# A two-FFN and state-space layer: the shared expert takes its turned operands from memory, where the router's are stored

## What is computed

```python
x = x + 0.5 * _L0_ffn_ref(_layernorm(x, axis=-1), ...)
x = x + _L0_attn_ref(_layernorm(x, axis=-1), ...)
x = x + 0.5 * _L0_ffn_ref(_layernorm(x, axis=-1), ...)
```

```python
logits = flat @ router_w.T
scores = jax.nn.softmax(logits, axis=-1)
_, topk_idx = jax.lax.top_k(logits + router_bias, K)
...
xg = flat[tok_table]
g = jnp.einsum('ecd,efd->ecf', xg, gate_w)
u = jnp.einsum('ecd,efd->ecf', xg, up_w)
y = jnp.einsum('ecf,edf->ecd', jax.nn.silu(g) * u, down_w)
out = jnp.zeros_like(flat).at[tok_table.reshape(-1)].add((y * w_table[..., None]).reshape(-1, d))
sg = jnp.einsum('nd,sfd->nsf', flat, sh_gate_w)
su = jnp.einsum('nd,sfd->nsf', flat, sh_up_w)
out = out + jnp.einsum('nsf,sdf->nd', jax.nn.silu(sg) * su, sh_down_w)
```

## Time and profile before

| | |
|---|---|
| time, median of 3 runs | 2375.12 us (2374.70 to 2375.79) |
| profiled execution, its own time | 2374.74 us |
| its span, first to last instruction | 2373.0 us |
| mean granted TensorE clock | 0.994 |
| VectorE busy | 1393.6 us (59%) |
| ScalarE busy | 950.3 us (40%) |
| GpSimd busy | 680.9 us (29%) |
| DMA, mean | 123 GB/s, 292.81 MB |

### The profile page before, as it was taken

The page is one execution under the profiler, slowest core; times in us unless marked ns, Lnnn a source line. Parts: engine busy times, 40 slices in busy tenths (PEclk is TensorE's granted clock), DMA queues, the critical chain, the costliest instruction groups (busy, mean ns, idle before and its releaser), DMA issues.

```text
span 2373.0 us, 41894 instructions
## 1 busy us (share of the span) xinstructions
PE 2328.0 (98%) x16700; PEld 2059.6 (87%) x16700; DVE 1393.6 (59%) x3240; ACT 950.3 (40%) x1650; POOL 680.9 (29%) x526
## 2 busy tenths in 40 slices
PE   6999999999999999999999999999999999999997
PEld 6999999777788899998998898998999999877787
DVE  6777762223228777777777777778777763222221
ACT  5333322333327455554545555455433232323331
POOL 1244443111220323232322222321144444112121
PEclk9999999999999999999999999999999999999999
DMA  8644213899844111111111111104263411799958
GB/s 265 205 144 153 86 64 126 261 279 282 253 93 133 36 36 28 28 28 28 27 28 27 28 27 28 28 19 161 74 222 109 141 65 37 254 289 287 276 106 176
DMA packets 102785, 292.81 MB, mean 123 GB/s; under 512 B 22530, under 2 KB 22786, under 8 KB 91904
## 3 DMA queue, kind: packets, MB, share of 16 engines
q1 hardware_dynamic: 55248, 198.87, 23.3%
q0 software_dynamic: 47344, 91.27, 17.3%
HBM read 197.28 MB, written 151.80 MB: 147 GB/s over the span
## 4 chain that ended last, share of the span: by engine, by line
PE 96%; DVE 2%; ACT 1%; issue 1%; DMA 0%; DVEq 0%; POOL 0%; SPq 0%; ACTq 0%
PE m_p_ab L1614 5%; PE m_p_ab L1615 5%; PE m_p_ab L1616 5%; PE m_p_x L1616 3%; PE m_p_x L1615 3%; PE m_p_x L1614 3%; PE p_up_b L713 3%; PE p_up_a L713 3%; PE p_gate_a L713 3%; PE p_up_b L715 3%; PE p_up_b L714 3%; PE p_gate_b L713 3%; PE p_gate_a L715 3%; PE p_gate_a L714 3%; PE p_up_a L715 3%; PE p_up_a L714 3%
## 5 line engine op out<-in xcount | busy, mean ns | idle before, releaser
L1927 DVE SCALAR_TENSOR_TENSOR m_xt<-m_ssm,m_convw,m_xt 128x256 f32<-128x256 f32 x384 | 219.1, 584 | 58.1 <-ACT m_ssm L1483 48.9
L459 POOL DMA_INDIRECT slot_rows<-a_hr,a_slot_now x128 | 130.4, 1019 | 152.1 <-PE p_gate_a L715 96.5
L459 POOL DMA_INDIRECT slot_rows<-b_hr,b_slot_now x128 | 130.3, 1018 | 151.8 <-PE p_gate_b L715 96.5
L1614 PE MATMUL m_p_ab<-m_ht_hi,m_wi_b_hi 128*128 128x256 f32 x576 | 163.6, 284 | 3.3 <-ACT m_gate L1455 3.3
L1615 PE MATMUL m_p_ab<-m_ht_lo,m_wi_b_hi 128*128 128x256 f32 x576 | 161.7, 281 | 0.0
L1616 PE MATMUL m_p_ab<-m_ht_hi,m_wi_b_lo 128*128 128x256 f32 x576 | 161.7, 281 | 0.0
L713 PE MATMUL p_gate_a<-a_hts_hi,a_w_hi 128*128 128x256 f32 x512 | 149.4, 292 | 1.7 <-DVE a_hts_lo L1009 1.4
L713 PE MATMUL p_up_a<-a_hts_hi,a_w_hi 128*128 128x256 f32 x512 | 147.9, 289 | 0.0
L713 PE MATMUL p_gate_b<-b_hts_hi,b_w_hi 128*128 128x256 f32 x512 | 147.4, 288 | 0.3
L713 PE MATMUL p_up_b<-b_hts_hi,b_w_hi 128*128 128x256 f32 x512 | 147.7, 288 | 0.0
L1389 POOL TENSOR_TENSOR m_state_dec<-m_state,m_etot 128x1024 f32<-128x1024 f32 x31 | 74.0, 2387 | 255.4 <-ACT m_etot L1499 255.4
(11 more groups left out here) (374 smaller groups left out, 7518.8 us busy)
## 6 DMA issues: line engine op xcount, KB each, us to landing
a_ew<-in_ew SPq DMA_DIRECT2D x32, 1536.0 KB, 7.6
b_ew<-in_ew SPq DMA_DIRECT2D x32, 1536.0 KB, 7.3
after_ffn<-a_zeros POOLq DMA_DIRECT2D x6, 2048.0 KB, 9.2
out<-b_zeros POOLq DMA_DIRECT2D x6, 2048.0 KB, 9.2
slot_rows<-a_zeros POOLq DMA_DIRECT2D x1, 8336.0 KB, 40.0
a_rows<-slot_rows SPq DMA_DIRECT2D x32, 260.5 KB, 8.0
b_rows<-slot_rows SPq DMA_DIRECT2D x32, 260.5 KB, 8.1
a_xs<-in_x SPq DMA_DIRECT2D x16, 512.0 KB, 4.2
```

What stands on the lines that cost most here:

```text
L459: g_.indirect_dma_start(out=xg, out_offset=bass.IndirectOffsetOnAxis(ap=slot_now[r % HR][:, at:at + 1], axis=0), in_=hr[r % HR][:, j, :], ...
L1614: t.matmul(out, l_hi, r_hi_, start=first, stop=False)
L1927: ins_ = v.scalar_tensor_tensor(xt[:, m, :], ssm[:, m, i:i + BM], convw[:, m, i:i + 1], xt[:, m, :], ALU.mult, ALU.add)
```

## The change

The router's halves of the turned rows, htr_hi and htr_lo, are stored to a new tensor in memory, `turned`, piece by piece (`store_turned`, two DMAs of 256 KB for each of four pieces of each routing block, in runs of 1 KB). For blocks 1 to 15 SP loads hts_hi and hts_lo from there (`load_turned`, two DMAs of 512 KB for each block). hs, its turns and splits remain for block 0 alone. ScalarE's copy to htr_hi waits until both stores of the piece two before have landed. The final read of the second FFN and `finish` now wait for `xs_loaded`. One tensor and three semaphores are new.

```diff
+            def store_turned(r, k):
+
+                for i, (part, ready) in enumerate(((htr_hi, htr_hi_ready), (htr_lo, htr_ready))):
+                    sp.wait_ge(ready, r * KD + k + 1)
+                    sp.dma_start(turned[2 * r:2 * r + 2, :, i, k * BS:(k + 1) * BS].rearrange("b p t -> p b t"),
+                                 part[:, k % 2, :].bitcast(F32).rearrange("p (b t) -> p b t", b=2)).then_inc(turned_stored[k % 2], 16)
+
+            def load_turned(b):
+                for v in range(2):
+                    sp.wait_ge(turned_stored[v], 32 * (KD // 2) * (b // 2 + 1))
+                if b >= 2:
+                    sp.wait_ge(up_full, (b - 1) * UN)
+                for i, part in enumerate((hts_hi, hts_lo)):
+                    sp.dma_start(part[b % 2][:, :, :].bitcast(F32).rearrange("p k t -> p (k t)"),
+                                 turned[b, :, i, :]).then_inc(hts_loaded, 16)
...
                         sp.dma_start(xr[:], src_r[b + 1]).then_inc(xr_loaded, 16)
+                    if b < NR:
+                        store_turned(b, 0)
                     if 1 <= b <= NR + 1:
                         sp.wait_ge(acc_ready, b * TS)
                         sp.dma_start(acc_s[b - 1], xs[:, (b - 1) % XB, :, :]).then_inc(x_stored, 16)
+                    if b < NR:
+                        for k in range(1, KD):
+                            store_turned(b, k)
+                    if b + 1 < NS:
+                        load_turned(b + 1)
...
-                pool.wait_ge(hs_mid, NS * TS)
+                pool.wait_ge(xs_loaded[(NS - 1) % XB], 16 * ((NS - 1) // XB + 1))
...
                 act.wait_ge(tr_full, f + 1)
                 if f >= 2:
                     act.wait_ge(lt_done, f - 1)
+                    act.wait_ge(turned_stored[k % 2], 32 * (f // 2))
                 a.activation(htr_hi[:, k % 2, :], p_x0[:], ACT.Copy).then_inc(htr_hi_ready, 1)
...
-                        if more and u == 2:
-                            turned_s(b + 1, 0)
-                        if more and u == 3:
-                            turned_s(b + 1, 1)
...
-                        if more and u == 1:
-                            normed(b + 1)
...
-                if g == 0 and u == 0:
-                    pe.wait_ge(hts_ready, 2 * b + 2)
+                if g == 0 and u == 0 and b == 0:
+                    pe.wait_ge(hts_ready, 2)
+                if g == 0 and u == 0 and b > 0:
+                    pe.wait_ge(hts_loaded, 32 * b)
...
-                        if more and u == 3:
-                            turn_s(b + 1, 1)
...
-                        if more and u == 2:
-                            turn_s(b + 1, 0)
...
-                if b == 0 and not prior:
-                    dve.wait_ge(xs_loaded[0], 16)
+                dve.wait_ge(xs_loaded[b % XB], 16 * (b // XB + 1))
...
-                sp.wait_ge(prior.ts_full, 2 * NS)
+                sp.wait_ge(prior.ts_full, 2)
```

More of the change, by code:

```diff
@@ L268, in ffn @@
         xs_loaded, x_stored = [sem(f"xs_loaded{u}") for u in range(XB)], sem("x_stored")
+        turned_stored, hts_loaded = [sem(f"turned_stored{u}") for u in range(2)], sem("hts_loaded")
         hs_mid, hs_ready, ts_full = sem("hs_mid"), sem("hs_ready"), sem("ts_full")
@@ L295, in ffn @@
                  hr[2][:, :, :].rearrange("p j d -> p (j d)")[:, 0:PIECE]]
-        turned_in = lambda b, half: p_gate if b == 0 and half == 1 else p_ts
+        turned_in = p_ts, p_gate
         norms = lambda at: at // TS + 1 if at < TR else at // TR + 2
@@ L674, in program @@
                         i, g = b * UN + u, b * POS + 3 * u
-                        routes, more = b < NR, b + 1 < NS
+                        routes = b < NR
                         gate_silu(i)
@@ L715, in three, with turn_s @@
                 return t.matmul(out, l_lo, r_hi_, start=False, stop=last)
[L717 to L720, removed]
+            def turn_s(half):
+                pe.wait_ge(hs_ready, TS)
                 for kk in range(2):
@@ L723, in turn_s @@
                     for j in range(TS):
-                        mm = t.matmul(turned_in(b, half)[:, kk, j * P:(j + 1) * P], hs[:, j, k * P:(k + 1) * P], c.ident[:],
+                        mm = t.matmul(turned_in[half][:, kk, j * P:(j + 1) * P], hs[:, j, k * P:(k + 1) * P], c.ident[:],
                                       is_transpose=True, start=True, stop=True)
@@ L1005, in assign_weights, with turned_s @@
                 link(v.tensor_tensor(chosen_before[:], chosen_before[:], chosen_sum[:], ALU.add))
-            def turned_s(b, half):
-                dve.wait_ge(hts_hi_ready, 2 * b + half + 1)
-                v.tensor_tensor(hts_lo[b % 2][:, 2 * half:2 * half + 2, :], turned_in(b, half)[:, :, :],
-                                hts_hi[b % 2][:, 2 * half:2 * half + 2, :].bitcast(F32), ALU.subtract).then_inc(hts_ready, 1)
+            def turned_s(half):
+                dve.wait_ge(hts_hi_ready, half + 1)
+                v.tensor_tensor(hts_lo[0][:, 2 * half:2 * half + 2, :], turned_in[half][:, :, :],
+                                hts_hi[0][:, 2 * half:2 * half + 2, :].bitcast(F32), ALU.subtract).then_inc(hts_ready, 1)
             def product(i):
@@ L2098, in build @@
         after_mamba = nc.dram_tensor("after_mamba", (T, D), F32).ap()
+        turned = nc.dram_tensor("turned_rows", (NS, P, 2, KD * BS), F32).ap()
         xg = nc.dram_tensor("slot_rows", (SLOTS, ROW), F32).ap()
@@ L2104, in build @@
         with Phase(nc) as s:
-            first = ffn(nc, "a", c, s, ins["x"], after_ffn, xg, *weights, 0, True, False)
+            first = ffn(nc, "a", c, s, ins["x"], after_ffn, xg, turned, *weights, 0, True, False)
             state_space = first.follow = mamba(nc, c, s, after_ffn, after_mamba, ins, first)
```

65 lines of the change are left out of this document (29 added, 36 removed).

## The result

The changed kernel takes 2409.99 us (median, 2406.47 to 2417.98) against 2375.36 us of the kernel before in the same comparison: ratio 1.0135, 95% interval 1.011 to 1.0161. The forecast was 2375.6 us with a range up to 2392; the time lies 18 us above that range. The profiled execution took 2413.4 us, span 2411.7, 38.7 us more than the span before.

The account below looks back on a forecast made before the run. Bound: TensorE (98% busy), with the add chain and full-DMA tail ending within a few us of it. Terms -22.0 + 2.0 + 8.1 + 1.2 + 4.7 + 1.5 + 5.0 = +0.5 on the 2375.1 median gave 2375.6 us, range 2358 to 2392.

Parts of the forecast that it names:

- the pairs of the first FFN: Expert pairs, first FFN: slowed adds hold ScalarE's copy 8.6 us, 7 covered, leaving 1.5 us, bounds 0 and 8.6.
- What is removed: Shared expert's transposes on TensorE: 0.44 us a group; 50 groups count, 22.0 us gained of 26.4.
- The twelve steady blocks: Steady routing blocks: waits for the stores behind the row load stall 2.0 us together, bounds 0 and 10.
- Block 0 of the second FFN: TensorE's fourth turn there waits for the k=0 stores: 5.4 us stall plus 2.7 of lost clock, 8.1 together.
- Blocks 0 and 1 of the first FFN: Late stores cost 1.2 us in block 0; clearing and new traffic cost 4.7 in block 1, bounds 1 and 10.
- The cover: First FFN's pairs: ScalarE's next product is wanted nearly one pair's time (7.7 us) later, hiding an estimated 7 us.
- The adds of the second FFN: Chain of adds, second FFN: five new 1 MB loads at 0.9 us per MB cost 5.0 us, bounds 0 and 19.
- Slower by the adds: Rival, expert pairs: each 1 MB load holds the adds 2.85 us, 14.2 instead of 5.0 for five; 2394.0 us, chance 0.25.
- Stores in time: Rival, routing blocks: stores are not held behind the row load, so ScalarE never waits; 2359.6 us, chance 0.22.
- TensorE alone: Rival, whole kernel: adds are not slowed, the tail shrinks with TensorE, all 26.4 us come; 2348.7 us, chance 0.06.
- Loads late: Rival, block starts: TensorE waits for loaded operands, 16 routing-block loads late by 1 us each; 2391.6 us, chance 0.05.

Follow-up runs that it names:

- only_removed: Changed kernel with blocks 2 to 15 neither turned nor loaded and no stores, reusing the operands of blocks 0 and 1: 2357.8 us, 0.9905 of the kernel before.
- stores_only: As only_removed, plus the stores of routing blocks 1 to 7 and ScalarE's wait for them, no loads: 2357.17 us, 0.9915 of the kernel before.
- the third buffer: Changed kernel with three instead of two buffers for the router's halves, so a copy waits for the stores three pieces before: 2405.24 us, 1.0098.
- small_clear: Changed kernel with only an eighth of the slot rows cleared (1 MB instead of 8336 KB): 2399.21 us, 1.0092 of the kernel before.
- outside_the_pairs: Changed kernel loading operands for blocks 2 to 9 only, routing blocks 0 and 5 to 7 storing nothing, k=0 stores ahead of the row load: 2380.01 us, 1.0003.
- loads_only: As only_removed, plus full-size loads for blocks 2 to 15 from the rows routing block 1 stored, the only block storing: 2382.98 us, 1.0008.
- loads_2_to_9: As outside_the_pairs, but with the row load ahead of the k=0 stores, as in the changed kernel: 2365.99 us, 0.9949 of the kernel before.

## Why the prediction was wrong, point by point

The terms of the sum beside the stages of the changed kernel: 6.9 against 21.5 up to the first pair add, 1.5 against 13.8 in the pairs of the first FFN, 9.1 against 9.6 in the third stage, 5.0 against 14.9 in the adds of the second, and 0.9 in the tail. Three terms were too small, by 14.6, 12.3 and 9.9 us.

- **What is removed: right.** 0.44 us a group was predicted; only_removed gave 8.2 us where 7.9 were due, twice. 
- **The twelve steady blocks: small, as predicted.** 2.0 us were predicted; stores_only shows 1.2 and 3.1 us for seven blocks each, some 4 us in all, inside the bounds 0 to 10 and of the size of the scatter.
- **Block 0 of the second FFN: right.** Predicted: the fourth turn stalls 5.4 us, 8.1 with the clock. Measured: 4.96 us, at 1689.96; the third buffer takes back 7.0. The terms as written (1664.7, 0.6, 0.7 and 0.15) give 1666.1 and not 1666.4, a stall of 5.1 us, which is nearer still. The stage lost 9.6 where 8.1 + 1.0 were in the sum. The reading of the earlier trace rows, stores take the place of the transfer behind the row load, was sound.
- **Blocks 0 and 1 of the first FFN: the step that failed first.** The sum had 1.2 + 4.7 (with 1.0 for the steady blocks 6.9 in this stage), bounds up to 10 for the two blocks, and 21.5 were lost. Three faults. I let the stores of k=0 land at 39.0 like the load in the earlier trace rows; they landed at 43.3, and in four other kernels with the same order at 39.9 to 44.5. With the clearing issued at 34.4, while they are on their way, or without it, this differs little, so the cause of this part stays open. I costed only the wait of piece 2; piece 3 waits for the stores of k=1, the second of which is issued after the clearing, and which took 19 us (8.49 us on ScalarE, 5.6 on TensorE). And I placed the clearing's harm in block 1, where ScalarE had no such wait, the clearing being over at 78.4 (34.4 + the 44.0 us to its landing). The earlier trace rows gave the clearing's duration; its start I never read. small_clear gives 15.3 us of the 21.5 to it.
- **The pairs of the first FFN: mechanism seen, size wrong.** I wrote that the adds hold the ScalarE copy, 8.6 us, of which 7 are covered. In the run ScalarE waited 61.9 us in 15 places, the longest 12.3. The cover, "nearly one pair's time", exists once: the delays add up until all five buffers are full, and from then on each goes to TensorE. 8.7 us of idle and 5.0 of clock, 13.8 instead of 1.5. With the whole loads beside them these pairs take 311.7 to 316.9 us in seven kernels, without loads 302.3 to 307.5 in five, and 319.1 in outside_the_pairs.
- **The adds of the second FFN: size wrong.** 5.0 us were predicted for 5 MB, from 0.9 us per MB in the earlier trace rows. The stretch there holds 26 distances and not 27, 7.7 us each, which makes 1.0 us per MB: the miscount is not the fault. Measured: 14.9 in the changed kernel, 3.0 us beside each load. That step compared adds under a steady 278 GB/s with adds under 48; the price of a further MB on engines already 90% busy is not that average: 20.7 us for 5 MB in loads_only against stores_only, 4.1 a MB. The upper bound of 19, each MB stops the chain for the time that it takes to move, was the nearer end. The Trainium skill, "DMA: Bandwidth & Descriptors", section "Queues, rings and completion order", has each engine take turns between its queues; by that I had worked out 9.4, still too little.
- **The rivals.** "Slower by the adds" was right in its mechanism and near in its price: 2.85 us a load assumed, 3.0 measured, 14.2 against 14.9 for the second FFN. That it fits so closely is partly luck, for other pairs of kernels give 3.8 to 5.0 us a load (18.8 to 24.8 us for five). Had it been the forecast, 2394.0, most of what is missing to 2410 is the first block (14.6). "Stores in time" nearly holds for the steady blocks (ScalarE waits 0.5 to 2.7 us in eight places, TensorE at most 1.1), and for block 0 of neither FFN. "TensorE alone" would be 2348.7; in the traces of only_removed and of the changed kernel the end follows the adds and not TensorE, which speaks against it. "Loads late" came true in one place, 3.4 us beside the clearing.
- **The chances.** Slower had 0.35, with blocks 0 and 1 bounded at 10. The unseen part was a second wait of the same kind, beside the clearing, and the clock after the stalls: 6.5 us of it here and 5.0 in the pairs, while the sum had 2.7 for one stall.

## What to carry to other kernels

Before traffic is added to a stage, read two things in its trace: which large transfers are under way there, with their start as well as their length, and which chain of dependent transfers runs beside it. Where the DMA engines are 90% busy and such a chain is as long as the compute, price each added MB at the time that it takes to move, on the chain, and again on the compute once the buffers between them are full; leave such loads out, as loads_2_to_9 does. Where a buffer can be overwritten only when a store has landed, follow each of its next uses, not just the first, and count the clock behind each stall.

## What the runs showed of the hardware

- A pair of 256 KB stores issued behind a 1 MB load and 2 us ahead of a clearing of 8336 KB landed after 10.9 us, the next pair, whose second store was issued behind the clearing, after 19, against a median of 3.5 and 4.2 us for the 32 stores of each half in the first FFN. The Trainium skill, "DMA: Bandwidth & Descriptors", section "Anatomy of one DMA", gives the fit by which 2.6 us were estimated for transfers of the GpSimd queue, and these stores go on SP's; it describes none of them here: even the median is above it.
- Without any load beside it the chain of adds still took from 258.8 to 269.3 us in six kernels whose adds and weights are the same; with the whole loads it took 275.7 to 283.6 in seven.
- The lost clock is about half of the stalls: for 23.9 us of additional idle in the first 150 us and in the stretch 550 to 650, 11.5 us more of clock.
- The order of transfers in one queue (two 256 KB stores, with the wait for their data, ahead of or behind a 1 MB load) moved the stage before the first add by 4.4 us and the third by 3.7, in favour of the large one first.
